# Attention over a context with a routed FFN: the probability product with the probabilities as weights, and a fifth transposing DMA

## The chip, the cores and the metric

The kernel runs on one core of one Trainium2 chip. The time is device microseconds of one execution, from its start to its end. The core has five engines with queues of their own: TensorE (PE; its weight loads are listed as PEld), VectorE (DVE), ScalarE (ACT), GpSimd (POOL) and SyncE (SP), which here only issues DMAs. They wait for one another by semaphores.

## What is computed

Sixteen batches of 128 tokens of width 512; each batch has its own context of 128 tokens of width 256. 32 heads of width 16. The attention, cut to what matters:

```python
q = (layernorm(x) @ Wq).reshape(b, n, 32, 16)
k, v = split(ctx @ Wkv, 2)
q, k = apply_axial_rope(q, pos), apply_axial_rope(k, pos)
w = softmax(einsum('bqhd,bkhd->bhqk', q, k) / 4)
attn = einsum('bhqk,bkhd->bqhd', w, v).reshape(b, n, 512)
x = x + attn @ Wout + bout
x = x + ffn(layernorm(x))     # one shared expert, 16 routed ones, two for each token
```

## The kernel before, in words

The kernel works in fp32 accuracy. Large products are split in two fp16 parts (high and low) of each factor and need three fp16 matmuls (`product`, L501, with `PARTS`); so each matrix that is a factor exists as a high part (made by ScalarE, `..._high`) and a low part (what is left, made by GpSimd or VectorE, `..._low`). The scores are made of such parts as well, with the parts stacked in 64 rows. Only the product of probabilities and values is made in fp32 matmuls.

A batch passes through these parts:

- `ln1_stats`, `ln1_norm` (VectorE), `rstd1_make` (GpSimd), `xn_transpose` (TensorE, L489), `xnT_copy`, `xnT_low`.
- `project_k`, `project_v`, `project_q` (TensorE, L508 to L538), in pieces of three matmuls of 512 columns each: two pieces for K and for V, four for Q. K and Q share the PSUM bank `p_qk`, V and the output projection share `p_v`.
- `k_turn`, `k_sum`, `q_turn`, `q_sum` (VectorE): the rotation. `k_high`, `q_high` (ScalarE), `k_low`, `q_low` (GpSimd) write the fp16 parts in rows, and SP turns them in four transposing DMAs a batch (`turn_parts`, L419), into `kT` and `qT`.
- `scores` (L540, four calls), from which VectorE takes the negative maximum over the keys for each query (`row_max`, L1079, eight calls). `negmax_transpose` (L555) turns them, `neg_copy` copies them, and `shifted_scores` (L564, four calls) makes the scores again, now with keys in the partitions and queries in the free dimension, the maximum taken off by a further matmul. `exp` (ScalarE, L807, eight calls of four heads) writes the fp32 probabilities to `prob`, a ring of four.
- `weigh_values` (L579, four calls of eight heads). The weights of the array are the values of a head, 32 columns wide (16 of them the head's, 16 zeros, in `vpad`), the moving side is `prob`, 128 keys by 128 queries; so the result has the head's dimension in the partitions. Four products for different column groups stand beside each other in the array. As many products again, with `sum_row` as weights, give the sums of the probabilities. ScalarE copies the half (`summed_v_copy`, L813), VectorE inverts the sums (`sums_invert`, L1094), TensorE spreads the inverses over the 16 rows of each head (`spread_recip`, L600, two fp32 matmuls with 128x128 weights) and VectorE multiplies (`normalise`, L1100). So `attn` is already turned, and `attnT_high`, `attnT_low` split it for `project_out` (L606).
- `residual`, `ln2_stats`, `ln2_norm`, `xn2_high`, `xn2_low`, `xn2_transpose`, `xn2T_copy`, `gate_logits`, `keep_logits`: the second norm and the logits of the experts; both forms are stored to DRAM for the FFN.

Every engine has its own loop over steps (`pipeline`, L304), and in it a list, `step(b, on)`, that is written out by hand: `on(d, part)` does the part for batch b + d. So the engines' queues are interleavings of four to six batches in a fixed order, and what is written earlier in an engine's list holds up what comes after it. The lists of TensorE (L643), ScalarE (L881), VectorE (L1169), GpSimd (L1456) and SP (L433) are replaced by the change.

After the attention the eight shared and the routed tiles of the FFN follow (`pair`); the gate and up products of the first shared tile stand in TensorE's last attention step. `project_out(B - 1)` and `hidden_transpose` come behind it. In the last steps ScalarE and VectorE also split the shared weights.

Of the kernel before, what the change touches and what calls it, by code (L numbers as in the profile page):

```python
# [23 lines left out]
F16 = mybir.dt.float16  # L24
# [3 lines left out]
ALU = mybir.AluOpType  # L28
# [3 lines left out]
B = 16  # L32
# [48 lines left out]
def build(nc, x, ctxT, pos, wq, wkv, wo, bout, gateT, gbias, s13, s2, e13, e2, out):  # L81
    with ExitStack() as stack:
# [58 lines left out]
        recip = sb("recip", [P, P])  # L141
        summed_v = sb("summed_v", [P, 2, 3 * P])
        attn = sb("attn", [P, 2, 2 * P])
        attnT = sb("attnT", [P, 2, KC, P], F16)
# [77 lines left out]
        pv_sum = p_pv[:, 2 * P:3 * P]  # L222
# [13 lines left out]
        cleared = sem("cleared"); ident_ready = sem("ident_ready"); consts = sem("consts"); zeroed = sem("zeroed")  # L236
# [16 lines left out]
        pv_done = sem("pv_done"); summed_v_kept = sem("summed_v_kept"); recip_ready = sem("recip_ready")  # L253
        spread_done = sem("spread_done"); attn_ready = sem("attn_ready")

        attnT_hi = sem("attnT_hi"); attnT_lo = sem("attnT_lo"); gate_parts = sem("gate_parts")
# [22 lines left out]
        v_part = vpad.rearrange("p b (m a) d -> p b m (a d)", a=2)  # L279
        v_part = bass.AP(v_part.tensor, v_part.offset, [v_part.ap[0], [HEADS * 2 * HD, 2], [4 * HD, PAIRS], [3 * HD, 2], [1, HD]])  # L280
        attn_rows = attn[:].rearrange("p a n -> p (a n)").rearrange("p (c t) -> p c t", t=P)
# [105 lines left out]
        def _(sp):  # L387
# [44 lines left out]

            def step(b, on):  # L433
                on(-2, turn_k_parts, 0)
                on(-2, turn_q_parts, 0)
                on(-5, store_xn2)
                on(1, load_ctx)
                on(-2, turn_k_parts, 1)
                on(-5, store_xn2T)
                on(-2, turn_q_parts, 1)  # L440
# [47 lines left out]
        def _(pe):  # L488
# [90 lines left out]
            def weigh_values(b, par, i):  # L579

                if i == 0:
# [3 lines left out]
                    else:  # L585
                        pe.wait_ge(consts, 1)
# [3 lines left out]
                block = slice(i % 2 * P, (i % 2 + 1) * P)  # L590
# [950 lines left out]
```

## Time and profile before

| | us |
|---|---|
| median of three timed runs | 694.45 (lowest 692.33, highest 1107.32) |
| the profiled execution | 689.33 |
| its span, first to last instruction | 687.5 |
| TensorE busy | 635.5 (92%) |
| VectorE busy | 503.2 (73%) |
| ScalarE busy | 368.9 (54%) |
| GpSimd busy | 332.9 (48%) |

The profile and the trace tell of one execution. "Busy" is the time in which an engine has an instruction under way; matmuls are pipelined, so it isn't the time in which the array is full. The granted clock is TensorE's, as a share of 2.4 GHz; 0.50 is 1.2 GHz. The attention takes the first 325 us, the FFN the rest.

### The profile page before, as it was taken

What the parts mean: (1) busy time and instruction counts of PE and PEld (TensorE: products, weight loads), DVE (VectorE), ACT (ScalarE), POOL (GpSimd) and SP (SyncE); (2) the same over time, 40 slices, a digit from 0 to 9 for tenths busy, and PEclk for the clock granted to TensorE, in tenths of its full rate; (3) what the DMA queues carried; (4) which work ended last, traced back from release to release, by engine and by line L of the source; (5) the groups of instructions that cost most, each with busy time, mean ns of one, the idle gap of its engine ahead of it and who ended that gap; (6) DMA issues with size and microseconds to landing.
All of it is one profiled execution on the core that took longest, in us unless ns stands there. A gap on an engine that the chain in (4) does not pass through costs nothing.

```text
span 687.5 us, 19434 instructions
## 1 busy us (share of the span) xinstructions
PE 635.5 (92%) x7104; PEld 406.6 (59%) x7104; DVE 503.2 (73%) x976; ACT 368.9 (54%) x620; POOL 332.9 (48%) x390
## 2 busy tenths in 40 slices
PE   2769999999999999988999999999998999999992
PEld 1346666666666666656566566666665666666661
DVE  8779888888888888866486935776765676666671
ACT  4255655666565666566411115665664666666660
POOL 3524555555555555432000012468565478777661
PEclk9989999999999999999999999999999999999997
DMA  9824744544444445650322662665877954555942
GB/s 316 222 48 64 176 112 97 88 94 94 99 99 99 99 99 122 93 125 33 123 92 62 217 210 87 197 197 92 210 219 196 279 111 92 100 85 151 262 77 33
DMA packets 105279, 90.63 MB, mean 132 GB/s; under 512 B 71632, under 2 KB 75728, under 8 KB 105232
## 3 DMA queue, kind: packets, MB, share of 16 engines
q1 hardware_dynamic: 91600, 59.76, 33.4%
q0 software_dynamic: 8752, 20.71, 15.5%
q10 hardware_dynamic: 4880, 9.52, 4.1%
q8 instruction: 31, 0.51, 0.3%
q14 instruction: 16, 0.13, 0.1%
HBM read 69.85 MB, written 22.81 MB: 135 GB/s over the span
## 4 chain that ended last, share of the span: by engine, by line
PE 79%; DMA 5%; DVE 5%; issue 4%; POOL 2%; ACT 2%; SPq 2%; POOLq 0%; ACTq 0%; DVEq 0%
PE p_sc L724 14%; PE p_qk L693 13%; PE p_sc L693 12%; PE p_qk L504 8%; PE p_v L504 8%; PE p_pv L593 4%; PE p_pv L596 3%; DMA used_twice_too<-used_twice 3%; PE p_tr L687 2%; PE p_pv L711 2%; PE p_sc L552 2%; PE p_pv L603 2%; PE p_sc L573 2%; PE p_sc L576 1%; SPq L425 1%
## 5 line engine op out<-in xcount | busy, mean ns | idle before, releaser
L1085 DVE TENSOR_REDUCE negmax<-p_sc 128x4 f16<-128x512 f32 x128 | 79.4, 684 | 6.0 <-PE p_sc L552 4.6
L933 ACT CAST hiddenT<-p_pv 128x384 f16<-128x384 f32 x54 | 25.9, 479 | 107.0 <-PE p_pv L711 103.2
L811 ACT ACTIVATE prob<-p_sc 128x512 f32<-128x512 f32 x128 | 66.1, 602 | 20.2 <-PE p_sc L576 19.9
L1491 POOL DMA_INDIRECT out<-prob,to_at x38 | 69.4, 1826 | 11.1 <-issue 9.7
L724 PE MATMUL p_sc<-used_twice,hiddenT 128*128 128x512 f16 (+1 forms) x306 | 71.7, 379 | 0.9 <-DVE hiddenT L1215 0.9
L1471 POOL COPY from_at<-from_rows 128x1 uint32 (+1 forms) x40 | 33.1, 828 | 80.8 <-DVE from_rows L1330 77.4
L693 PE MATMUL p_qk<-used_twice,xeT 128*128 128x352 f16 x420 | 68.4, 313 | 0.5 <-DMA xeT<-xn2T_dram 0.5
L693 PE MATMUL p_sc<-used_twice,xeT 128*128 128x352 f16 x420 | 68.4, 312 | 0.0
L1211 DVE TENSOR_TENSOR hidden<-p_sc,act_g 128x352 f32<-128x352 f32 x55 | 28.8, 524 | 52.5 <-PE p_sc L693 32.0
L920 ACT COPY xeT<-p_tr 128x1024 f16<-128x1024 f16 x40 | 40.5, 1012 | 37.4 <-PE p_tr L687 35.8
L504 PE MATMUL p_qk<-used_twice,xnT 128*128 128x512 f16 x192 | 52.1, 399 | 6.4 <-DVE swp L1063 6.4
L593 PE MATMUL p_pv<-prob,used_twice_too 128*32 128x128 f32 x1024 | 53.5, 279 | 3.0 <-ACT prob L811 1.8
L1228 DVE TENSOR_SCALAR prob<-p_sc,gate_at 128x512 f32<-128x512 f32 x38 | 28.5, 751 | 37.6 <-PE p_sc L724 30.5
L1442 POOL TENSOR_TENSOR used_twice<-rot,used_twice 128x1024 f16<-128x1024 f32 x16 | 34.2, 2136 | 43.6 <-ACT used_twice L798 43.6
L693 PEld LDWEIGHTS p_sc<-used_twice,xeT 128*128 128x128 f16 x420 | 41.0, 98 | 21.4
L596 PE MATMUL p_pv<-prob,sum_row 128*32 128x128 f32 x1024 | 52.5, 275 | 0.0
L693 PEld LDWEIGHTS p_qk<-used_twice,xeT 128*128 128x128 f16 x420 | 40.8, 98 | 19.4 <-DMA xeT<-xn2T_dram 0.7
L504 PE MATMUL p_v<-used_twice,attnT 128*128 128x512 f16 x192 | 48.9, 380 | 2.6 <-POOL attnT L1450 2.6
L1476 POOL DMA_INDIRECT xe<-xn_dram,from_at x40 | 44.7, 1117 | 8.2 <-issue 4.5
L724 PEld LDWEIGHTS p_sc<-used_twice,hiddenT 128*128 128x128 f16 (+1 forms) x306 | 29.0, 98 | 30.8 <-issue 1.3
L1454 POOL TENSOR_TENSOR xn_parts<-xn,xn_parts 128x512 f16<-128x512 f32 x16 | 18.9, 1179 | 52.9 <-ACT xn_parts L838 52.9
L724 PE MATMUL p_sc<-used_twice_too,hiddenT 128*128 128x512 f16 (+1 forms) x180 | 43.3, 386 | 0.0
(180 smaller groups left out, 1463.6 us busy)
## 6 DMA issues: line engine op xcount, KB each, us to landing
w<-e SPq DMA_DIRECT2D x20, 1408.0 KB
w<-e SPq DMA_DIRECT2D x20, 512.0 KB
out<-stream SPq DMA_DIRECT2D x17, 256.0 KB, 2.0
xn_dram<-xn_parts SPq DMA_DIRECT2D x16, 256.0 KB, 2.2
xn2T_dram<-xn2T SPq DMA_DIRECT2D x16, 256.0 KB, 2.5
w<-e SPq DMA_DIRECT2D x20, 192.0 KB
stream<-x ACTq DMA_DIRECT2D x1, 3584.0 KB, 18.0
xeT<-xn2T_dram ACTq DMA_DIRECT2D x14, 256.0 KB, 2.7
```

The lines of the kernel that those rows point to most:

```text
L504: mm = pe.matmul(to, rows[:, r_part, c, :], w[:, w_part, c, :], start=(c == 0 and r_part + w_part == 0), stop=(c == last and r_part == 1))
L593: pe.matmul(p_pv[2 * HD * n:2 * HD * (n + 1), block], vpad[:, par, head(c, n), :], prob[:, c % RING, n * P:(n + 1) * P], start=(c % 4 == 0 ...
L596: mm = pe.matmul(pv_sum[2 * HD * n:2 * HD * (n + 1), :], sum_row[:, c % 4, :], prob[:, c % RING, n * P:(n + 1) * P], start=False, stop=(c ...
L693: mm = pe.matmul(p_out, xeT[:, u, x_part, c, :], w[:, w_part, c, at:at + INNER], start=(c == 0 and x_part + w_part == 0), stop=(c == KC - ...
L724: mm = pe.matmul(p_y[u][:], hiddenT[0:k, h_part, c, :], w[0:k, w_part, c, :], start=(c == 0 and h_part + w_part == 0), stop=(c == len(ICH) ...
L811: act.activation(prob[:, c % RING, :], p_scored(c)[:], ACT.Exp, scale=SCALE).then_inc(exp_ready, 1)
L920: act.copy(xeT[:, u], p_xT).then_inc(sems.xeT_ready, 1)
L1085: dve.tensor_reduce(negmax[:, c % 2, at:at + CH], p_scored(c)[:].rearrange("p (h t) -> p h t", t=P), AX_X, ALU.max, negate=True).then_inc( ...
L1442: pool.tensor_tensor(q_part[:, :, :, 1, :], twice_each(rot[:, 0:DIM]), q_part[:, :, :, 0, :], ALU.subtract).then_inc(q_parts, 1)
L1471: pool.tensor_copy(from_at[:, par, u:u + 1], from_rows[:, bass.ds(q, 1)]).then_inc(from_copied, 1)
L1476: pool.indirect_dma_start(out=xe[:, u].rearrange("p a d -> p (a d)"), out_offset=None, in_=xn2_dram, in_offset=bass.IndirectOffsetOnAxis(a ...
L1491: pool.indirect_dma_start(out=out, out_offset=bass.IndirectOffsetOnAxis(ap=to_at[:, par, u:u + 1], axis=0), in_=ye[:, par, u], in_offset=N ...
```

## The change

The probabilities become the weights of the array: for each head `prob` (128 keys x 128 queries, fp32) is loaded, and the values of the head with a column of ones, 17 columns (`v_one`), move through. The result `p_heads` has the queries in the partitions, and for each head 16 values and the sum of its probabilities. The products with `sum_row`, `spread_recip` and `summed_v_copy` are gone; VectorE inverts 16 sums a half and multiplies with them spread by the access pattern. `attn` now is in rows; its two fp16 parts (`attn_high` on ScalarE, `attn_low` on GpSimd) are turned by a fifth transposing DMA on SP (`turn_attn`), into one of two buffers of `attnT`. All five lists are written anew. The gate and up products of the first shared tile move behind TensorE's loop.

```diff
-        vpad = used_twice_too[:, 0:4 * DIM].rearrange("p (b h d) -> p b h d", b=2, h=HEADS)
-        sum_row = sb("sum_row", [P, 4, 2 * HD])
-        spread_to = sb("spread_to", [P, 2, P])
+        v_one = used_twice_too[:, 0:2 * HEADS * (HD + 1)].rearrange("p (b h d) -> p b h d", b=2, h=HEADS)
...
+            def turn_attn(b, par):
+                sp.wait_ge(attn_lo, b + 1)
+                if later(b, 2):
+                    sp.wait_ge(wo_done, b - 1)
+                sp.nop().then_inc(turning, 1)
+                sp.dma_start_transpose(attnT[:, par].rearrange("p a c t -> p (a c) t"), attn_parts[:].rearrange("p a d -> p (a d)")).then_inc(attnT_ready, 16)
...
+                on(-3, turn_q_parts, 0)
+                on(-3, turn_k_parts, 1)
                 on(1, load_ctx)
+                on(-3, turn_q_parts, 1)
...
+                on(-5, store_xn2)
+                on(-4, turn_attn)
+                on(-2, turn_k_parts, 0)
+                on(-5, store_xn2T)
...
                 for c in (2 * i, 2 * i + 1):
                     for n in range(CH):
-                        pe.matmul(p_pv[2 * HD * n:2 * HD * (n + 1), block], vpad[:, par, head(c, n), :], prob[:, c % RING, n * P:(n + 1) * P],
-                                  start=(c % 4 == 0), stop=(c % 2 == 1), skip_group_check=True)
-                    for n in range(CH):
-                        mm = pe.matmul(pv_sum[2 * HD * n:2 * HD * (n + 1), :], sum_row[:, c % 4, :], prob[:, c % RING, n * P:(n + 1) * P],
-                                       start=False, stop=(c % 4 == 3), skip_group_check=True)
+                        mm = pe.matmul(p_heads[:, head(c, n) % HALF, :], prob[:, c % RING, n * P:(n + 1) * P], v_one[:, par, head(c, n), :], start=True, stop=True)
                 mm.then_inc(pv_done, 1)
-
-            def spread_recip(b, par, half):
-                pe.wait_ge(recip_ready, b * 2 + half + 1)
-                for n in range(2):
-                    mm = pe.matmul(p_pv[:, n * P:(n + 1) * P], spread_to[:, n, :], recip[:], start=True, stop=True)
-                mm.then_inc(spread_done, 1)
...
             def project_out(b, par, c):
                 if c == 0:
-                    pe.wait_ge(attnT_lo, b + 1)
+                    pe.wait_ge(attnT_ready, b * 16 + 16)
...
```

TensorE's list afterwards, whole:

```python
on(-2, scores, 3)
on(-4, gate_logits)
on(0, xn_transpose)
on(-1, project_v, 1)
on(0, project_k, 0)
on(0, project_k, 1)
on(-3, project_out, 0)
on(-2, negmax_transpose)
on(-3, project_out, 1)
on(-2, shifted_scores, 0)
on(-2, shifted_scores, 1)
on(-3, project_out, 2)
on(-3, project_out, 3)
on(-2, shifted_scores, 2)
on(-2, weigh_values, 0)
on(-2, weigh_values, 1)
on(-2, shifted_scores, 3)
on(0, project_q, 0)
on(-2, weigh_values, 2)
on(-2, weigh_values, 3)
on(0, project_q, 1)
on(-1, scores, 0)
on(-3, xn2_transpose)
on(-1, scores, 1)
on(0, project_q, 2)
on(0, project_q, 3)
on(0, project_v, 0)
on(-1, scores, 2)
```

The others afterwards, shortened to their order (batch offsets of each engine's own step in brackets):

```text
ACT   xnT_copy(-1), v_copy(-2), q_high(-2), exp 0..7(-3), xn2_high(-4), gate_act(0) in step B+2,
      attn_high(-3), xn2T_copy(-4), k_high(-1), ctx_high(0), keep_logits(-4)
DVE   q_sum(-3), neg_copy(-4), ln1_norm(-1), k_turn(-2), residual(-5), ln2_stats(-5),
      sums_invert 0(-4), normalise 0(-4), ln2_norm(-5), k_sum(-2), ln1_stats(0),
      sums_invert 1(-4), normalise 1(-4), split of wo in step 2, row_max 0..3(-3), q_turn(-2),
      row_max 4..7(-3), xnT_low(-1)
POOL  k_low(-2), ctx_low(-1), rstd1_make(0), q_low(-2), bias_add(-3), rstd2_make(-4),
      xn2_low(-4), attn_low(-3)
```

VectorE's part of the product afterwards:

```diff
             def sums_invert(b, par, half):
-                dve.wait_ge(summed_v_kept, b * 2 + half + 1)
+                dve.wait_ge(pv_done, b * 4 + (2 * half + 2))
...
-                dve.reciprocal(recip[:], summed_v[:, half, 2 * P:3 * P]).then_inc(recip_ready, 1)
+                dve.reciprocal(recip[:].rearrange("p (h o) -> p h o", o=1), p_heads[:, :, HD:HD + 1]).then_inc(recip_ready, 1)
 
             def normalise(b, par, half):
-                dve.wait_ge(spread_done, b * 2 + half + 1)
+                dve.wait_ge(recip_ready, b * 2 + half + 1)
...
-                dve.tensor_tensor(attn[:, half], p_pv[:, 0:2 * P], summed_v[:, half, 0:2 * P], ALU.mult).then_inc(attn_ready, 1)
+                dve.tensor_tensor(attn[:, half].rearrange("p (h d) -> p h d", d=HD), p_heads[:, :, 0:HD],
+                                  recip[:].rearrange("p (h o) -> p h o", o=1).broadcast_to([P, HALF, HD]), ALU.mult).then_inc(attn_ready, 1)
```

## Rows read from the trace of the kernel before

**Rows 1.** Windows: one step; busy us (count) by engine, clock, DMA share, GB/s.

```profile
160.00:177.55 17.55, 17.49 (x301) 11.35 (x296) 15.75 (x36) 10.75 (x19) 9.78 (x8) 1.00 0.41 91
```

**Rows 2.** Timeline of TensorE in one step: start us, us, instruction, count.

```profile
163.71 0.61 PE L603 MATMUL p_pv<-recip,spread_to 128*128 128x128 f32 x4
164.25 0.62 PE L552 MATMUL p_sc<-used_twice_too 64*128 64x128 f16 x16
164.81 0.46 PE L504 MATMUL p_tr<-gate,xn2T 128*128 128x16 f16 x12
165.12 0.81 PE L504 MATMUL p_v<-used_twice,ctx 128*128 128x512 f16 x3
...
177.04 0.43 PE L593 MATMUL p_pv<-prob,used_twice_too 128*32 128x128 f32 x8
...
178.92 1.47 PE L504 MATMUL p_qk<-used_twice,xnT 128*128 128x512 f16 x6
```

**Rows 3.** Groups of weight loads, shapes apart: count, busy us, mean ns, idle before.

```profile
L603 PEld LDWEIGHTS p_pv<-recip,spread_to 128*128 128x128 f32 x128 | 17.8, 190 | 10.6 <-DVE recip L1098 8.6
...
L596 PEld LDWEIGHTS p_pv<-prob,sum_row 128*32 128x32 f32 x1024 | 31.6, 111 | 0.0
```

**Rows 4.** Timeline of weight loads where TensorE had been idle: one load; four loads.

```profile
314.20 0.19 PEld L603 LDWEIGHTS p_pv<-recip,spread_to 128*128 128x128 f32 x1 [1.54 <-DVE recip L1098]
...
314.20 0.52 PEld L603 LDWEIGHTS p_pv<-recip,spread_to 128*128 128x128 f32 x4 [1.54 <-DVE recip L1098]
```

**Rows 5.** Timeline of TensorE and VectorE between the two kinds of scores.

```profile
169.59 0.23 PE L573 MATMUL p_sc<-used_twice_too 64*128 64x128 f16 x2
...
176.49 0.62 PE L552 MATMUL p_sc<-used_twice_too 64*128 64x128 f16 x16
...
179.57 0.95 DVE L1098 RECIPROCAL recip<-summed_v 128x128 f32<-128x128 f32 x1 [0.16 <-ACT summed_v L817]
...
181.97 0.42 DVE L1104 TENSOR_TENSOR attn<-p_pv,summed_v 128x256 f32<-128x256 f32 x1 [0.18 <-PE p_pv L603]
...
186.66 0.23 DVE L1092 COPY negmaxT<-p_tr 128x128 f16<-128x128 f16 x1 [0.68 <-PE p_tr L562]
```

**Rows 6.** Groups from 100 to 250 us, and landing of the transposing DMAs.

```profile
L1446 POOL TENSOR_TENSOR used_twice<-rot,used_twice 128x1024 f16<-128x1024 f32 x8 | 17.1, 2138 | 1.2 <-ACT used_twice L805 0.5
...
L1450 POOL TENSOR_TENSOR attnT<-attn,attnT 128x512 f16<-128x512 f32 x8 | 9.3, 1159 | 1.0
...
L805 ACT CAST used_twice<-rot 128x1024 f16<-128x1024 f32 x8 | 8.4, 1048 | 0.0
...
L830 ACT COPY xn2T<-p_tr 128x1024 f16<-128x1024 f16 x8 | 8.1, 1012 | 0.7
...
L1394 POOL TENSOR_TENSOR ctx<-ctx_sb,ctx 128x256 f16<-128x256 f32 x8 | 5.4, 672 | 0.0
...
L823 ACT CAST attnT<-attn 128x512 f16<-128x512 f32 x8 | 5.0, 620 | 4.3 <-DVE attn L1104 4.3
...
DMA to landing us min/median/max: 3.0/3.2/4.8
```

**Rows 7.** Timeline of TensorE: first weighing of batches 0, 13, 15; last output projection.

```profile
45.44 0.65 PE L593 MATMUL p_pv<-prob,used_twice_too 128*32 128x128 f32 x8 [0.42 <-ACT prob L811]
...
277.41 0.43 PE L593 MATMUL p_pv<-prob,used_twice_too 128*32 128x128 f32 x8
...
309.86 0.42 PE L593 MATMUL p_pv<-prob,used_twice_too 128*32 128x128 f32 x8
...
322.63 2.76 PE L504 MATMUL p_v<-used_twice,attnT 128*128 128x512 f16 x12 [0.33 <-POOL attnT L1450]
```

**Rows 8.** Windows at the start and in a late step; columns as in rows 1.

```profile
36.00:42.50 6.50, 0.72 (x4) 0.11 (x2) 6.23 (x11) 2.98 (x7) 0.00 (x0) 0.86 0.00 0
...
45.40:47.20 1.80, 1.76 (x36) 1.79 (x40) 1.42 (x1) 0.87 (x2) 1.44 (x2) 0.50 0.54 104
...
294.20:309.90 15.70, 12.57 (x269) 8.96 (x271) 11.61 (x23) 10.23 (x19) 4.41 (x5) 1.00 0.65 136
```

More of the change, by code:

```diff
@@ L656, in step @@
-                on(-1, project_q, 0)
-                on(-3, spread_recip, 0)
-                on(-1, project_q, 1)
-                on(-2, scores, 0)
-                on(-2, scores, 1)
-                on(-3, weigh_values, 2)
-                on(-3, weigh_values, 3)
-                on(-1, project_q, 2)
-                on(-1, project_q, 3)
-                if isinstance(b, int) and b == B + 2:
-                    pe.wait_ge(turned_q, B * 3)
-                    pe.wait_ge(lo13, KC)
-                    gate(0, 0, 0, 0, "shared")
@@ L769, in pair @@
                             place()
-            pipeline(step, pe, 0, B + 2, 6, (B - 6) // 2, ahead=[xn_transpose])
+            pipeline(step, pe, 0, B + 1, 6, (B - 6) // 2, ahead=[xn_transpose])
+            pe.wait_ge(turned_q, B * 3)
+            pe.wait_ge(lo13, KC)
+            gate(0, 0, 0, 0, "shared")
+            pe.wait_ge(exp_ready, B * NCH)
+            up(0, 0, 0, 0, "shared")
+            gate_logits(B - 2, 0)
             for c in range(KC):
@@ L915, in step @@
                     split_shared13()
+                on(-2, q_high)
+                on(-3, exp, 0)
+                on(-3, exp, 1)
+                on(-3, exp, 2)
+                on(-3, exp, 3)
+                on(-3, exp, 4)
+                on(-3, exp, 5)
+                on(-3, exp, 6)
+                on(-3, exp, 7)
+                if isinstance(b, int) and b == B + 2:
+                    split_shared2()
+                on(-4, xn2_high)
+                if isinstance(b, int) and b == B + 2:
+                    gate_act(0)
+                on(-3, attn_high)
+                on(-4, xn2T_copy)
+                on(-1, k_high)
+                on(0, ctx_high)
+                on(-4, keep_logits)
             def xeT_copy(n, u):
@@ L1169, in step @@
             def step(b, on):
+                on(-3, q_sum)
+                on(-4, neg_copy)
+                if isinstance(b, int) and b == B + 3:
+                    split_shared13((0, 1))
+                on(-1, ln1_norm)
+                on(-2, k_turn)
+                on(-5, residual)
+                on(-5, ln2_stats)
+                if isinstance(b, int) and b == B + 3:
+                    split_shared13((2, 3))
+                on(-4, sums_invert, 0)
+                on(-4, normalise, 0)
+                on(-5, ln2_norm)
+                if isinstance(b, int) and b == B + 3:
+                    split_shared2()
+                on(-2, k_sum)
+                on(0, ln1_stats)
+                on(-4, sums_invert, 1)
+                on(-4, normalise, 1)
+                if isinstance(b, int) and b == 2:
+                    weights_low(wo16, wo_in, KC, KCC + KC)
+                    dve.wait_ge(gate_parts, 1)
+                    dve.scalar_tensor_tensor(gate16[:, 1], gate_sb[:], W_SCALE, gate16[:, 0], ALU.mult, ALU.subtract).then_inc(gate_parts, 1)
+                on(-3, row_max, 0)
+                on(-3, row_max, 1)
+                on(-3, row_max, 2)
+                on(-3, row_max, 3)
+                on(-2, q_turn)
                 on(-3, row_max, 4)
```

153 lines of the change are left out of this document (30 added, 123 removed).

## The prediction

> **What bounds the kernel now.** I read the windows first. In one full step of the attention loop (17.55 us, one batch) TensorE is busy 17.49 us, VectorE 15.75, ScalarE 10.75, GpSimd 9.78, and the granted clock is 1.00, that is 2.4 GHz [rows 1]. The first probability product of batch 0 starts at 45.44 and that of batch 15 at 309.86 [rows 7]: 264.42 us for 15 steps, 17.63 each. So the attention is a row of equal steps bound by TensorE, and VectorE is the next engine. What comes after it (shared and routed experts) isn't touched; it starts when the last output projection is done, so a shift there is taken along to the end.
>
> Then I read TensorE's own order inside a step. Two calls of `weigh_values` (half a batch: 16 products with values and 16 with `sum_row`, two matmul instructions each, 64 in all) run from 177.04 to 178.92: 1.88 us. One `spread_recip` runs from 163.71 to 164.25: 0.54 us [rows 2]. Three matmuls of 512 columns, one piece of a projection, take 3 x 512 columns at 2.4 GHz, 0.64 us, with gaps 0.65.
>
> **What is removed on TensorE.** Two halves at 1.88 and two spreads at 0.54: 4.84 us a batch.
>
> **What is added there.** 32 fp32 matmuls a batch, one for each head, whose weights are the probabilities (128x128) and whose moving side is 17 columns. The trace shows each fp32 matmul as two pairs of weight load and matmul (4 instructions of L603 for 2 matmuls in the source), so 64 pairs. A moving side of 17 columns is nearly nothing: 12 pairs with 16 columns in fp16 run from 164.81 to 165.12, 26 ns a pair [rows 2]. The price is the loading. There the type and the width count: an fp32 load of 128 columns lasts 190 ns, one of 32 columns 111 [rows 3]; the difference, 79 ns for 96 columns, is 0.82 ns a column, 105 ns for 128. The pace shows it directly: where the array had been idle and the loads of L603 began alone, the first load lasts 0.19 us and four of them 0.52, so they start (0.52 - 0.19)/3 = 0.11 us apart, and before the second no matmul was in the way [rows 4]. So 64 x 0.11 = 7.04 us a batch. Bounds: from below 26 ns a pair, as fp16 weights show (1.7 us a batch); from above 190 ns, if a load could not overlap the one before (12.2 us). I take 0.11 us, because it is measured on the same type and width. The old form had hidden this: it loaded 32 columns into one of four column groups at a time, and its instructions passed at 1.88/64 = 29 ns each.
>
> The Trainium skill, in "TensorE: Matmul & The Clock Gate", section "LDWEIGHTS (loading the stationary operand)", puts a load at its columns divided by 1.2 in ns, and its section "Weight-path perf modes" leaves fp32 out of the fast load. That would give 107 ns a load and 6.8 us a batch, against 7.0 by the row. It speaks against the change, since the same section's fast load is what makes 16-column matmuls cheap in fp16.
>
> **Sum on TensorE.** 17.5 - 4.84 + 7.04 = 19.7 us a step. The change takes away multiplications and gives back more in loads: +2.2 us.
>
> **Other engines.** VectorE loses two reciprocals of 128x128 at 0.95 [rows 5], and gets two of 128x16; between an eighth of that, 0.12, by the number of elements, and the old 0.95. I take 0.15; it stands in the rivals alone, since VectorE has slack. ScalarE loses the two copies of `summed_v`. Both had slack. SP gets a fifth transposing DMA: 3.2 us from issue to landing [rows 6]. GpSimd has the same work. None of this is on the path while it is hidden by TensorE; what could bring it there are the two loops that close over a step:
>
> First loop, by way of VectorE. The first shifted scores of a step start at 169.59, so those of the next one a step of 17.55 later, at 187.14; from the first scores (176.49) to them there are 10.65 us now. In this stretch the new order leaves out the reciprocal (0.95 and 0.16 of wait), the normalisation (0.42 and 0.18) and the 0.68 of idle before the copy of the maxima, since `q_sum` now stands there [rows 5]; instructions overlap by some 0.1, so about 8.5 remain. From the first shifted scores (169.59) to the next scores (176.49) there are 6.90 us; the new order has no spread (-0.54), all four weighings instead of the first two (-1.88 + 7.04) and one piece of output projection more (+0.65): 12.2. Together 20.7 us.
>
> Second loop, by ScalarE and GpSimd: after the last weighing come reciprocal and normalisation (together with the matmul's tail some 0.85), `attn_high` 0.62, `xn2T_copy` 1.01, `k_high` 1.05, `k_low` 2.14, `ctx_low` 0.67 [rows 6], and only then `project_k`, since `ctx_low` is now queued behind `k_low`. Together 6.3 us, then two pieces of K (1.3), two of the output (1.3) before the shifted scores, and from them to the end of the last weighing 11.0 (12.2 less the last piece of Q, 0.65, and the gaps): with 0.2 for the handing over 20.1 to 20.2.
>
> Three ways to count the step, 19.7, 20.2 and 20.7; each contains small gaps, the last the most. I take 20.2. The attention output's own chain, `attn_high` 0.62, `attn_low` 1.16, DMA 3.2 [rows 6], ends some 5.2 us after the last normalisation, thus 6.0 after the last weighing. Between the last weighing and `project_out` TensorE has three pieces of Q, two of V, two of K, four of scores, two transposes and the gate product, 6.9 us and its waits; so the new chain is hidden with 1 us to spare, and beyond that it costs what it is late.
>
> **Sum over the kernel.** Thirteen full steps at 20.2 against 17.84 (277.41 - 45.44 over 13) [rows 7]: +30.6. The last two steps lack the projections of a next batch and have idle time already (they take 32.45 us together), so I count +1.5 each: +3. The start: `q_turn` of batch 0 now waits behind the splitting of the output weights, which ScalarE does only after V of batch 0; bounds 0 and +6, since TensorE was busy for only 0.72 of the 6.50 us before its first shifted scores [rows 8]; I take +3, nearer to what VectorE's queue has to take over. The end: from the first weighing of batch 15 to its output projection there are 322.63 - 309.86 = 12.77 us; afterwards it is four weighings and one piece of scores 7.5, transposes and the gate product 2.4, `gate_act` 0.5 (it stands before `attn_high` on ScalarE), 0.62 + 1.16 + 3.2 and hops, 15.6: +2.9. Sum +39.5. On the profiled execution (689.33 us, 687.5 of them span) this is 728.8. The median of the timed runs (694.45) lies 5 us over the profiled execution, of which I count half: **731 us**.
>
> **Rivals.**
> 1. Faster. The two weight sets hide the loads, or the fp32 load runs at the fp16 pace of 26 ns. Then the weighing is 1.7 us, TensorE has 14.4 us of work, VectorE 15.75 - 1.6 = 14.1, and the loops fall to about 15.2: 15 x 2.3 = 35 less, 3 more at the start: about 660. For it: beside these loads the trace has only fp32 matmuls of 128 columns, which could themselves set a pace of about 0.11. Against it: they can't set the first of the three gaps, since the array was empty, and three gaps that make 0.33 together leave no room for a short first one [rows 4]; and the duration grows with the columns [rows 3]. It decides from 75 ns a load down (4.84/64). Chance 0.07.
> 2. No change: a pace between, 80 ns, adds 5.1 and the new order wins a few tenths back; 15 x 0.3 and start and end: about 698. Chance 0.08.
> 3. A wait in the new order: the fifth transposing DMA stands in SP's queue between `store_xn2` and the K transposes, waits there for `attn_low`, and `project_out` gets its rows late; one landing took 4.8 us [rows 6]. At 1.5 us a step more, +22: 752. For it: only 1 us of slack. Against it: the queue has nothing else due just then. Chance 0.15.
> 4. The clock. In a weighing the array would multiply for 17 columns once or twice, 7 to 14 ns at 2.4 GHz, in each 110. After the stretch in which TensorE had been busy for 0.72 of 6.50 us the granted clock was 0.50 (1.2 GHz), from 45.4 to 47.2, up to 4.7 us after the end of that stretch [rows 8]. If the two weighing stretches of a step, 3.5 us each, count as idle, each costs half of some 4 us: 2 x 2 x 15 = 60: 790. Against it: through the last steps, with TensorE busy 80% of the time, the clock stays at 1.00 [rows 8]. Chance 0.10.
>
> The same page of the Trainium skill, "TensorE: Matmul & The Clock Gate", Part 4, says that transposes don't count as activity for the gate; no run here shows how loads count. By that, rival 4 would be likelier than I put it.
>
> **How the numbers follow.** My forecast has 0.60; its own range is 712 to 748 (steps of 19.6 to 20.9, start and end from 0 to 10). Low end 708, high end 764: this takes in rival 3 and leaves out rivals 1, 4 and part of 2. A measurement of this kernel tells about 2% (14 us) from no change, so faster means under 680, slower over 708: faster 0.07, same 0.08, slower 0.85.
>
> **What would show it.** Right: 64 loads of 128 columns fp32 a batch, 190 ns each and 0.11 apart, a weighing quarter of 1.76 us where it was 0.94; a step of 20.2 us with VectorE under 80% busy; `project_k` waiting for `ctx` from GpSimd, or the shifted scores for VectorE's maxima, under 1 us a step. Wrong: a pace of loads under 75 ns; steps under 17.6; a granted clock of 0.50 inside the steps; or a wait for the DMA of the attention rows before the output projection above 1 us a step.

## The result, and where the time went

The change made the kernel slower by 30%: 900.29 us (median of 4 runs, 895.06 to 901.07) against 693.39, a ratio of 1.298 with an interval of 1.292 to 1.304. That is not the 731 that was forecast, and not in its range. The profiled execution took 900.32, of which 898.3 are span; the granted clock over the whole span is 0.86 where it was 0.98.

Below are the head, two bands and four groups of the page after the change. Columns of the groups: count, then busy us and mean ns, then the idle time of the engine before them and what ended it.

```profile
span 898.3 us, 17096 instructions
...
PE 770.2 (86%) x5952; PEld 508.7 (57%) x5952; DVE 493.1 (55%) x976; ACT 355.6 (40%) x588; POOL 328.3 (37%) x382
...
PE   4387788779777977969999889999999989999994
...
PEclk9768798788878875677678679999999989999997
...
L593 PEld LDWEIGHTS p_pv<-used_twice_too,prob 128*128 128x128 f32 x1024 | 146.6, 230 | 6.0 <-issue 1.3
...
L555 PE MATMUL p_sc<-used_twice_too 64*128 64x128 f16 x512 | 33.9, 290 | 73.2 <-DMA used_twice_too<-used_twice 72.4
...
L1077 DVE RECIPROCAL recip<-p_pv 128x16 f32<-128x16 f32 x32 | 8.2, 257 | 104.1 <-PE p_pv L593 104.1
```

Two things stand in it that the forecast's sum has at zero. In the first 24 of the 40 slices, which are the attention, the clock moves between 0.5 and 0.9. And the first scores of the steps (L555) waited 72.4 us for a DMA that brings the turned Q and K.

The windows between the marks of [rows 7] put the loss in its place: start, 13 steps, the last two steps, the last output projection's wait, and the rest. Columns: busy us (count) of the five engines, clock, DMA share, GB/s.

```profile
0.00:55.42 55.42, 25.29 (x147) 10.91 (x148) 37.08 (x81) 20.28 (x32) 17.60 (x31) 0.85 0.55 171
55.42:457.15 401.73, 331.16 (x2857) 227.98 (x2853) 196.27 (x434) 129.00 (x219) 122.63 (x102) 0.79 0.32 68
457.15:507.19 50.04, 46.41 (x409) 34.48 (x405) 21.41 (x48) 18.19 (x31) 13.04 (x11) 0.69 0.35 77
507.19:528.09 20.90, 17.45 (x128) 14.62 (x125) 7.11 (x17) 7.57 (x13) 3.63 (x3) 0.76 0.14 38
528.09:898.30 370.21, 349.88 (x2424) 220.75 (x2424) 231.20 (x399) 180.57 (x294) 171.41 (x237) 0.97 0.56 144
```

| stretch | before [rows 7] | after | more | forecast |
|---|---|---|---|---|
| start, to the first weighing | 45.44 | 55.42 | 10.0 | 3 |
| 13 steps | 231.97 | 401.73 | 169.8 | 30.6 |
| last two steps | 32.45 | 50.04 | 17.6 | 3 |
| to the last output projection | 12.77 | 20.90 | 8.1 | 2.9 |
| after it | 364.87 | 370.21 | 5.3 | 0 |

Nine tenths of the loss are the steps (187.4 of 210.8 us): 30.9 us each (401.73/13) instead of 17.84, where 20.2 was forecast.

Now one step. First TensorE's timeline; each line has the start, the length, the instruction and, in brackets, the idle time before it.

```profile
209.80 3.75 PE L593 MATMUL p_pv<-used_twice_too,prob 128*128 128x17 f32 x32
...
214.69 3.64 PE L593 MATMUL p_pv<-used_twice_too,prob 128*128 128x17 f32 x32
...
218.18 1.07 PE L507 MATMUL p_qk<-used_twice,xnT 128*128 128x512 f16 x3
...
222.90 0.81 PE L507 MATMUL p_v<-used_twice,ctx 128*128 128x512 f16 x3
...
229.75 1.22 PE L555 MATMUL p_sc<-used_twice_too 64*128 64x128 f16 x16 [6.05 <-DMA used_twice_too<-used_twice]
```

The weighing itself is what was forecast: 32 pairs in 3.64 to 3.75 us, 0.11 us a pair and little more. But then compare the projections: three matmuls of 512 columns have 0.81 in [rows 2], and so has V at 222.90; the same in Q at 218.18 take 1.07. The windows of the same stretch say why (the last six columns as above):

```profile
209.80:213.60 3.80, 3.80 (x41) 3.77 (x39) 1.37 (x6) 1.08 (x2) 0.55 (x1) 1.00 0.76 175
...
214.70:218.20 3.50, 3.50 (x34) 3.50 (x34) 1.68 (x6) 1.03 (x3) 1.16 (x1) 1.00 0.39 75
218.20:223.60 5.40, 5.40 (x38) 2.50 (x37) 3.76 (x7) 2.88 (x4) 1.93 (x2) 0.68 0.01 3
223.60:229.70 6.10, 0.11 (x1) 0.00 (x0) 0.85 (x3) 0.00 (x0) 2.48 (x3) 0.93 0.42 108
229.70:231.00 1.30, 1.25 (x19) 0.80 (x20) 0.60 (x1) 0.00 (x0) 0.00 (x0) 0.50 1.16 187
231.00:234.00 3.00, 2.55 (x20) 1.60 (x20) 2.31 (x5) 0.77 (x2) 0.00 (x0) 0.50 0.04 6
```

Read the clock beside TensorE's busy time. TensorE is counted busy for the whole of both weighings, yet the clock falls at their end, to 0.68 on the mean of the next 5.4 us, and comes back. Then TensorE stands for 6 us, and once more the clock is at 0.50 (1.2 GHz) for what follows.

The wait is explained by the chain of waits, start and length, one step of it without pieces under 0.15 us:

```profile
214.85 3.49 PE p_pv L593 x32
218.37 0.27 DVE recip L1077
218.66 0.44 DVE attn L1083
219.19 0.63 ACT attn_parts L804
219.89 1.15 POOL attn_parts L1422
221.04 1.75 issue
222.82 0.31 POOL used_twice L1418
223.13 1.78 issue
224.91 0.67 POOL ctx L1374
225.84 0.41 SPq L412
226.38 3.26 DMA used_twice_too<-used_twice
229.75 1.22 PE p_sc L555 x16
```

The chain says "issue" (the engine waited for nothing that the profile shows) where the timelines of ScalarE and GpSimd have more:

```profile
220.79 1.01 ACT L811 COPY xn2T<-p_tr 128x1024 f16<-128x1024 f16 x1 [0.98 <-PE p_tr L619]
222.82 2.13 POOL L1418 TENSOR_TENSOR used_twice<-rot,used_twice 128x1024 f16<-128x1024 f32 x1 [1.78 <-ACT used_twice L792]
```

`k_low` (L1418) is one instruction of 2.13 us, which the chain cuts in two, and it waited 1.78 us for `k_high` (L792). That stands in ScalarE's list behind `xn2T_copy` (L811), which waited 0.98 us for the transposes that TensorE makes after the weighing, one piece of Q and one call of `scores`. So the weighing's end leads by two branches, VectorE's and TensorE's own list, over ScalarE and GpSimd to `ctx_low` (L1374). What waits for it is not only `project_k` but SP: `load_ctx` of a later batch (L412) stands in SP's new list between `turn_k_parts 1` and `turn_q_parts 1`, and so the transpose of Q's second part, whose data are long there, is issued after it. With 3.26 us from issue to landing the scores come 6 us late. This is a loop over the step (scores, exponentials, weighing, `xn2_transpose` and `attn_high`, `xn2T_copy`, `k_high`, `k_low`, `ctx_low`, `load_ctx`, `turn_q_parts 1`, scores), so the delay isn't caught up.

### The profile page after: what moved, and what is told of

Read it like the earlier page. It is cut to its first block, busy times and chain, and to the rows that moved or that the text cites. A ratio compares the mean times of both kernels' runs of the same rounds, so it can differ in the third digit from the quotient of the medians.

```text
span 898.3 us, 17096 instructions
## 1 busy us (share of the span) xinstructions
PE 770.2 (86%) x5952; PEld 508.7 (57%) x5952; DVE 493.1 (55%) x976; ACT 355.6 (40%) x588; POOL 328.3 (37%) x382
## 4 chain that ended last, share of the span: by engine, by line
PE 68%; DMA 11%; issue 10%; POOL 5%; ACT 3%; DVE 2%; SPq 1%; POOLq 0%; ACTq 0%; DVEq 0%
PE p_pv L593 14%; PE p_sc L705 11%; PE p_qk L674 10%; PE p_sc L674 9%; PE p_v L507 7%; PE p_qk L507 5%; DMA used_twice_too<-used_twice 5%; PE p_sc L576 2%; DMA stream<-x 2%; PE p_sc L555 2%; PE p_tr L668 2%; PE p_pv L692 2%; PE p_sc L579 2%; DMA xeT<-xn2T_dram 2%; PE p_tr L499 1%
## 5 line engine op out<-in xcount | busy, mean ns | idle before, releaser
L593 PEld LDWEIGHTS p_pv<-used_twice_too,prob 128*128 128x128 f32 x1024 | 146.6, 230 | 6.0 <-issue 1.3
L593 PE MATMUL p_pv<-used_twice_too,prob 128*128 128x17 f32 x1024 | 146.8, 293 | 0.5 <-DVE attn L1083 0.5
L555 PE MATMUL p_sc<-used_twice_too 64*128 64x128 f16 x512 | 33.9, 290 | 73.2 <-DMA used_twice_too<-used_twice 72.4
L555 PEld LDWEIGHTS p_sc<-used_twice_too 64*128 64x128 f16 x512 | 21.5, 124 | 95.9 <-issue 60.9
L674 PE MATMUL p_qk<-used_twice,xeT 128*128 128x352 f16 x420 | 70.2, 318 | 2.3 <-DMA xeT<-xn2T_dram 2.3
L507 PE MATMUL p_qk<-used_twice,xnT 128*128 128x512 f16 x192 | 66.9, 487 | 4.1 <-DVE swp L1042 4.1
L1077 DVE RECIPROCAL recip<-p_pv 128x16 f32<-128x16 f32 x32 | 8.2, 257 | 104.1 <-PE p_pv L593 104.1
L1191 DVE TENSOR_TENSOR hidden<-p_sc,act_g 128x352 f32<-128x352 f32 x55 | 28.8, 524 | 57.8 <-PE p_sc L674 38.0
L507 PE MATMUL p_v<-used_twice,attnT 128*128 128x512 f16 x192 | 50.7, 399 | 5.1 <-DMA attnT<-attn_parts 4.4
L674 PEld LDWEIGHTS p_sc<-used_twice,xeT 128*128 128x128 f16 x420 | 41.1, 98 | 21.6
L1422 POOL TENSOR_TENSOR attn_parts<-attn,attn_parts 128x512 f16<-128x512 f32 x16 | 18.5, 1154 | 83.9 <-ACT attn_parts L804 83.9
```

The source lines that it names most:

```text
L507: mm = pe.matmul(to, rows[:, r_part, c, :], w[:, w_part, c, :], start=(c == 0 and r_part + w_part == 0), stop=(c == last and r_part == 1))
L555: mm = pe.matmul(p_scored(2 * cc + a)[:, n * P:(n + 1) * P], qT[rows, CH * cc + n, :], kT[rows, CH * cc + n, :], start=True, stop=True)
L593: mm = pe.matmul(p_heads[:, head(c, n) % HALF, :], prob[:, c % RING, n * P:(n + 1) * P], v_one[:, par, head(c, n), :], start=True, stop=True)
L674: mm = pe.matmul(p_out, xeT[:, u, x_part, c, :], w[:, w_part, c, at:at + INNER], start=(c == 0 and x_part + w_part == 0), stop=(c == KC - ...
L1191: dve.tensor_tensor(hidden[:, 0:INNER], p_u, act_g[:], ALU.mult).then_inc(sems.hidden_ready, 1)
```

## The experiments

The theories before the runs: A, the wait in SP's queue is the loss and the clock follows from the idle time it makes; B, the long loads with hardly a multiplication let the clock fall by themselves, wait or none; with, for the forecast's terms, questions of the order of the work and of the type of the loads.

**1. `load_ctx` at the end of SP's list.**

```diff
                 on(-3, turn_k_parts, 1)
-                on(1, load_ctx)
                 on(-3, turn_q_parts, 1)
...
                 on(-5, store_xn2T)
+                on(1, load_ctx)
```

> The changed kernel with one line moved: SP's load_ctx stands at the end of SP's list and no longer ahead of the second Q transposes, which waited there for ctx_low. Theory A (the queue is the cause, and the idle 6 us a step are what lowers the clock): the wait for the DMA before scores 2 is gone, steps of 20.2 us, granted clock 1.00 inside the steps, in all about 750 us. Theory B (the two weighing stretches lower the clock by themselves, because the array hardly multiplies there): the wait is gone, but the clock still falls to 0.50 after or inside a weighing stretch in each step, steps of 23 to 27 us, in all 790 to 840 us.

It took 844.64 us, 55.7 less and a little above what B expected, with the clock at 0.856, as in the changed kernel (0.861). TensorE waits for no turned Q any more and is busy 29.11 us of 30, and still its clock is 0.77 there:

```profile
150.00:180.00 30.00, 29.11 (x259) 20.49 (x258) 17.30 (x40) 11.04 (x20) 12.37 (x11) 0.77 0.40 74
```

The step is 26.6 us ((449.04 - 50.05)/15, first weighings). Where the clock is low inside the weighing, the loads suffer too. TensorE's timeline of this kernel, two successive weighings, and 2-us windows (busy, clock, DMA share, GB/s) of TensorE alone:

```profile
186.51 3.75 PE L593 MATMUL p_pv<-used_twice_too,prob 128*128 128x17 f32 x32
...
192.15 6.85 PE L593 MATMUL p_pv<-used_twice_too,prob 128*128 128x17 f32 x32
```

```profile
192.00:194.00 2.00, 2.00 (x11) 0.50 0.88 171
...
204.00:206.00 2.00, 2.00 (x30) 0.95 0.16 29
```

The same 32 pairs take 3.75 us at 1.00 and 6.85 at 0.50: 214 ns a pair instead of 110. Against the changed kernel the edit wins 5.4 us before the first weighing and 3.5 in each of the 15 steps (26.6 against (507.19 - 55.42)/15 = 30.1), and loses 2.5 behind them. Theory A falls as the whole: without the idle time the clock is as low as with it.

**2. The engines' lists of before, with the new product.** All five lists in the old order, no `spread_recip`; the four pieces of `project_out` stand behind the first two shifted scores, and `turn_attn` goes between `turn_k_parts 0` and `turn_q_parts 0` (SP's list, shortened):

```diff
             def step(b, on):
-                on(-3, turn_q_parts, 0)
-                on(-3, turn_k_parts, 1)
+                on(-2, turn_k_parts, 0)
+                on(-4, turn_attn)
+                on(-2, turn_q_parts, 0)
+                on(-5, store_xn2)
                 on(1, load_ctx)
...
```

> The new product and the fifth transposing DMA with the five lists of the kernel before; only the output projection is moved behind the first shifted scores, to give the DMA its 3 us, and the fifth DMA stands between K's and Q's first transposes. Theory A (new order is the cause): no long wait for a DMA, clock 1.00, steps of about 20 us by the loads alone, in all about 735 us. Theory B (the product lowers the clock in any order): steps of 23 to 27 us, in all 780 to 840 us.

904.97 us, with a clock of 0.848; both theories had less, 735 and 780 to 840, since neither counted a wait for the fifth DMA in this order. Here TensorE waits in most steps for the turned attention rows, as rival 3 had it (which I had named for the new order, where it doesn't occur):

```profile
205.35 4.15 PE L507 MATMUL p_v<-used_twice,attnT 128*128 128x512 f16 x12 [4.82 <-DMA attnT<-attn_parts]
```

So the new order does what it is for: it takes the fifth transpose off the path. With the old one the product costs as much as with the new one and its wait.

**3. The new order with the old product**, on the kernel before (`load_ctx` last; where `spread_recip` and the copies of `summed_v` go is my own placing):

```diff
+                on(0, project_q, 0)
+                on(-2, spread_recip, 0)
...
+                on(0, project_q, 2)
+                on(-2, spread_recip, 1)
+                on(0, project_q, 3)
```

> The kernel before with the five new lists (load_ctx last on SP), but its own product: 32-column weights, sum_row, spread_recip (between the first two pieces of Q, and after the third), summed_v_copy, no fifth DMA. Theory B (only the product is slow, the new order is harmless once load_ctx is out of the way): clock 1.00, steps of 17.5 to 18.5 us, 690 to 715 us. Rival (the new order is itself slower, its loops close later): steps over 19 us, over 720 us.

753.73 us, ratio 1.087 (1.080 to 1.095); the step is 21.6 us. My forecast for it missed, and the rival was right: the order loses time with the old product. TensorE is busy 44.35 of 50 us at a clock of 0.97; it waits for the reciprocal before the spreads and for `logits` before the transposes:

```profile
215.82 0.71 PE L603 MATMUL p_pv<-recip,spread_to 128*128 128x128 f32 x4 [1.59 <-DVE recip L1097]
...
219.78 0.63 PE L496 MATMUL p_tr<-ident,xn 128*128 128x128 f32 x4 [1.01 <-ACT logits L866]
```

It doesn't say what the order alone costs, since another placing of the spreads might wait less. It does show that the order isn't free when the product between is another.

**4. Twice the moving columns.** Each head's matmul takes 32 columns (its own 17 and what lies beside them, which nobody reads) instead of 17; on experiment 1.

```diff
-        v_one = used_twice_too[:, 0:2 * HEADS * (HD + 1)].rearrange("p (b h d) -> p b h d", b=2, h=HEADS)
+        v_one = used_twice_too[:, 0:2 * HEADS * 2 * HD].rearrange("p (b h d) -> p b h d", b=2, h=HEADS)
...
-        p_heads = p_pv[:, 0:HALF * (HD + 1)].rearrange("p (h d) -> p h d", d=HD + 1)
+        p_heads = p_pv[:, 0:HALF * 2 * HD].rearrange("p (h d) -> p h d", d=2 * HD)
```

> As e1_ctx_last, with 32 columns of values moving where 17 moved (the columns beyond the one of ones are not used): twice the multiplying for the same loads and the same waits. Theory A: as e1_ctx_last within 1%. Theory B: the stretch counts for more in the clock, so it falls less often or later, 10 to 60 us faster than e1_ctx_last; the same time would say that twice this little isn't enough, and would leave B standing only if the clock falls at the same places.

840.54 us, clock 0.858: the same. The mean load is 265 ns (269 in experiment 1), and the second weighing of a step again takes 6.9 us in all steps but one. The columns themselves are free, as they should be behind a load of 110 ns, and the clock is no better for 15 more of them.

**5. Loads in fp16.** Probabilities and values in fp16, on experiment 1:

```diff
-                        mm = pe.matmul(p_heads[:, head(c, n) % HALF, :], prob[:, c % RING, n * P:(n + 1) * P], v_one[:, par, head(c, n), :], start=True, stop=True)
+                        mm = pe.matmul(p_heads[:, head(c, n) % HALF, :], prob16[:, c % RING, n * P:(n + 1) * P], v_one[:, par, head(c, n), :], start=True, stop=True)
```

> As e1_ctx_last, with probabilities and values rounded to fp16 (the low parts of both are left out), so that a head's product is one load and one matmul in fp16 instead of two and two in fp32. Both theories: a pair takes 26 to 30 ns, the weighing 1 us a batch instead of 7, the clock stays at 1.00, steps of 15.5 to 17 us by VectorE and the loops, in all 655 to 690 us. If the new order alone were slow, it would stay over 700.

690.54 us, 154 less than experiment 1 and just above the 655 to 690 expected. The timeline of TensorE and a window of this kernel:

```profile
207.48 0.56 PE L594 MATMUL p_pv<-used_twice_too,prob 128*128 128x17 f16 x16
```

```profile
180.00:210.00 30.00, 27.21 (x359) 15.12 (x357) 26.29 (x61) 19.27 (x33) 17.88 (x15) 1.00 0.50 114
```

Sixteen products in 0.56 us, 35 ns each with the end of the last one, where the fp32 form has 32 pairs in 3.75; and the clock is 1.00 in the window. The whole loss hangs on the type of the product, which sets both how long a load takes and how many there are. This isn't the changed kernel made whole again, since the low parts of the products are left out.

**6. A filler: more work, to hold the clock.** On experiment 1, behind each head's product one matmul of 240 columns of zeros in fp16, into columns of `p_pv` that nobody reads: 512 more matmuls.

```diff
                         mm = pe.matmul(p_heads[:, head(c, n) % HALF, :], prob[:, c % RING, n * P:(n + 1) * P], v_one[:, par, head(c, n), :], start=True, stop=True)
+                        mm = pe.matmul(p_pv[:, 512 - 240:512], ident16[:], filler[:], start=True, stop=True)
```

> As e1_ctx_last (844.6 us), with a matmul more behind each head's product: 128x128 weights in fp16, 240 columns of zeros moving, written beside the heads' results and read by nobody; 512 matmuls more in all. It runs while the next fp32 weights are loaded. Theory B (the weighing lowers the clock because the array hardly multiplies in it): the clock stays at 1.00 in the steps, a head takes 0.24 to 0.33 us instead of 0.22 at full and 0.43 at half clock, steps of 21 to 24 us instead of 26.6, in all 750 to 800 us: more work, less time. Rival (the fp32 loads themselves or the power lower the clock): the clock falls as before and the filler only adds, 850 to 880 us.

771.86 us: 72.8 less than the same kernel without the 512 matmuls. The windows of the steps, and the loads:

```profile
150.00:200.00 50.00, 49.11 (x579) 35.19 (x577) 32.58 (x79) 22.66 (x38) 21.33 (x18) 1.00 0.49 94
200.00:250.00 50.00, 48.66 (x588) 33.98 (x586) 34.99 (x81) 22.89 (x40) 22.79 (x20) 1.00 0.38 84
```

```profile
L594 PEld LDWEIGHTS p_pv<-used_twice_too,prob 128*128 128x128 f32 x1024 | 135.5, 195 | 5.2 <-issue 1.6 <-DVE attn L1085 1.2
```

The clock is 1.00, the mean load 195 ns over the whole kernel (269 in experiment 1, and [rows 3] have 190), and the step 21.7. The rival, that the fp32 loads or the power lower the clock, expected 850 to 880 and falls. The filler also brings 512 loads of its own, in fp16; experiment 10, which has the same loads and differs from this one in the moving columns alone, shows that more moving columns by themselves win 34.4 of the 72.8 us; how the rest divides between the filler's loads and its first 128 columns isn't shown. With both, theory B stands as the cause of the clock's part: how much the array multiplies between the loads.

**7. A lighter start**, on experiment 5: the splitting of the output weights moved to the end of step 2 on ScalarE, and to step 3 on VectorE (VectorE's part of the edit).

```diff
-                if isinstance(b, int) and b == 2:
+                if isinstance(b, int) and b == 3:
                     weights_low(wo16, wo_in, KC, KCC + KC)
```

> As e5_fp16 (690.5 us; low parts of probabilities and values left out), with the splitting of the output weights moved back behind the first batch's work on ScalarE (to the end of step 2) and VectorE (to step 3). If what e5 loses at its start (its first weighing at 51.7 us, before at 45.4) comes from that splitting: first weighing near 47, in all 684 to 687 us. If it comes from something else: as e5 within 2 us.

695.07 us, ratio to the kernel before 1.007 (1.002 to 1.012). The first weighing starts at 54.24, later than the 51.74 without the edit. But the experiment doesn't clear the splitting, since the edit moved it from one place on the path to another. TensorE's timeline, then VectorE's:

```profile
27.56 1.46 PE L508 MATMUL p_qk<-used_twice,ctx 128*128 128x512 f16 x6 [3.78 <-DVE swp L1043]
...
44.26 0.61 PE L556 MATMUL p_sc<-used_twice_too 64*128 64x128 f16 x8 [4.68 <-DVE negmax L1065]
...
38.62 4.16 DVE L1026 SCALAR_TENSOR_TENSOR used_twice<-w,used_twice 128x512 f16<-128x512 f32 x4 [5.17 <-ACT used_twice L832]
```

In experiment 5 the same wait for `q_turn` (L1043) is 7.19 us and the first scores start at 38.55; here it is 3.78 and they start at 35.26. So the splitting ahead of `q_turn` does cost 3.3 us of the start. Then it is paid back: the splitting now stands ahead of the first `row_max`, waits there 5.17 us for ScalarE's part of it, and the next scores wait 4.68 us for the maxima.

**8. The kernel before, with fp16 probabilities, values and `sum_row`**; low parts left out as in experiment 5.

```diff
-        vpad = used_twice_too[:, 0:4 * DIM].rearrange("p (b h d) -> p b h d", b=2, h=HEADS)
-        sum_row = sb("sum_row", [P, 4, 2 * HD])
+        vpad = used_twice_too[:, 0:2 * DIM].bitcast(F16).rearrange("p (b h d) -> p b h d", b=2, h=HEADS)
+        sum_row = sb("sum_row", [P, 4, 2 * HD], F16)
```

> The kernel before, its order and its form of the product, with probabilities, values and sum_row in fp16 (the low parts of probabilities and values are left out). It is the fair partner of e5_fp16: what the same rounding brings where 32-column weights stand beside each other. The product falls from 3.8 to about 1 us a batch on TensorE, so VectorE's 15.75 us bound the step: 16 to 16.6 us a step, in all 665 to 678 us, faster than before and than e5_fp16 (690.5). Rival (the old order's loop by way of VectorE sets the step, not TensorE): steps of 17 to 17.5, 685 to 692 us.

684.29 us, ratio 0.990 (0.985 to 0.994). The forecast was lower and the rival nearly right. The windows show whose limit comes next:

```profile
150.00:200.00 50.00, 46.75 (x686) 26.34 (x686) 45.68 (x103) 32.67 (x57) 28.52 (x25) 1.00 0.45 102
```

TensorE has some 3 us of 50 free, and VectorE is busy 45.68 of them: 91%. The old product leaves VectorE near its limit. Experiment 5 has taken VectorE's two large reciprocals away and its 15 steps take 16.8 us each ((303.96 - 51.74)/15; from batch 7 on 16.3), shorter than these 17.1; what it wins there it pays at the start, where its first weighing comes 5.4 us later (51.74 against 46.31), and at the end. Of all versions only this one is measurably faster than the kernel before, by 1%, at the price of precision.

**9. The filler on the changed kernel itself**, with `load_ctx` where the change has it. The edit is that of experiment 6.

> The changed kernel (900.3 us, load_ctx where the change put it) with the filler of e6_filler. Theory B with the wait as a second, separate cause of lost clock: the fall behind the second weighing is gone, the one after the idle 6 us stays, steps of 21.7 + 6 + 1 to 3 = 29 to 30.5 us against 30.9, in all 870 to 895 us. Rival (the idle time alone never lowers the clock, only idle time and weighing together): clock 1.00 throughout, steps of 27.5 to 28, 845 to 860 us.

871.64 us. The time is where theory B with a second cause had it (870 to 895), the steps a little over its 29 to 30.5. The wait for the turned Q is there again, up to 6.9 us long, and the steps with it are 30.7. The clock through the wait, TensorE alone:

```profile
218.00:220.00 2.00, 2.00 (x29) 1.00 0.00 0
220.00:222.00 2.00, 1.58 (x8) 1.00 0.00 0
222.00:224.00 2.00, 0.00 (x0) 0.96 0.00 0
224.00:226.00 2.00, 0.00 (x0) 0.50 0.21 63
```

After the weighing, the filler holds the clock at 1.00 (0.68 without it); through the idle time it can't, and it falls all the same. The steps to batch 9 take as long with the filler as without (first weighing of batch 9 at 330.97 and 332.38). In batch 5 one sees why: from the first weighing to the end of the second the filler takes 9.4 us instead of 8.5, and from there to the scores 10.6 instead of 11.4; TensorE's own work in between is shorter, and its wait longer by some of that (6.58 instead of 6.05). It wins only behind that: the changed kernel's next two steps take 37.1 and 35.4 us at clocks of 0.63 and 0.71, those with the filler 30.8. The last four steps have no wait in either kernel, since no context is left to load, and there the filler wins 4.1 us a step (21.5 against 25.6).

**10. A smaller filler**, 128 columns instead of 240, otherwise experiment 6.

> As e6_filler (771.9 us) with 128 filler columns for each head where 240 moved. Theory B, if this much multiplying still holds the clock: a head takes no longer than in e6_filler (0.25 us) and perhaps 0.24, clock 1.00 in the steps, 764 to 772 us. If it doesn't hold it: the clock falls in the steps again, and the time lies between e6_filler and e1_ctx_last, 790 to 840 us.

806.28 us, half way between 771.86 and 844.64, with steps that alternate between 21.6 and up to 27.7 us:

```profile
200.00:250.00 50.00, 49.10 (x516) 35.88 (x515) 28.97 (x68) 20.75 (x36) 19.02 (x16) 0.86 0.37 81
```

In some steps the clock falls, in others it holds.

## Why the prediction was wrong

The four kernels with and without the wait, with and without the filler, are the answer in one table (us):

| | `load_ctx` in the middle | at the end |
|---|---|---|
| no filler | 900.29 | 844.64 |
| filler | 871.64 | 771.86 |

Three of these are single runs; the kernel before took 692.98, 693.18 and 690.78 beside them, and from their last weighing on, where the four do nearly the same work, they take between 384.0 and 389.1 us, so differences of tens of us don't come from the chips. The two causes aren't additive: one remedy alone wins 55.7 or 28.7, both together 128.4. Each makes the clock fall, and while one of them is there the other's remedy is partly idle. By the step: 17.6 us before; with the loads at full clock 20.8; with the fall of the clock 26.6; with the wait 30.7 (batches 1 to 9; 30.9 over the first 13 steps, 30.1 over all 15). The 20.8 is experiment 6's 21.7 less the filler's own time: 14 heads took 3.48 us there (209.00 to 212.48), 0.249 each against 0.22 for two loads, so 32 x 0.029 = 0.9; that is an estimate, and no run has the loads at full clock without a filler.

Point by point:

- **The price of a load, 0.11 us: right.** 64 x 0.11 = 7.04 a batch; the trace after has 3.75 and 3.64 for its halves, and the duration is the 190 ns of [rows 3] where the clock is full. Rival 1 (loads hidden) falls. Rival 2 (80 ns) too.
- **The step at that price, 20.2: nearly right**, if the clock and the queue had been as the sum took them: 20.8. For the whole kernel experiment 6 gives an estimate: 771.86 less the filler's 16 x 0.9 is 757, inside the range of the forecast, some 26 above its value.
- **The first step that failed: the clock.** The sum multiplied durations of the full clock throughout, and the clock stood outside it as rival 4 with 0.10. Its mechanism is what happened: the weighing counts for little, and what follows runs at half the clock. Two things made me put it low. I took the last steps of before, with TensorE at 80% and a clock of 1.00 [rows 8], as the nearest row; but there the busy time is mostly multiplying, and in a weighing of 17 columns it is mostly loading. And the price I gave (2 us for each weighing, 4 a step, 790 in all) left out that the load itself slows down with the clock: a weighing at 0.50 takes 6.85 us instead of 3.75, 3.1 more. Measured it is 5.8 us a step (26.6 less 20.8). A page of the Trainium skill, "TensorE: Matmul & The Clock Gate", has in its section "HAM oscillation — how this bites in real kernels" the case of a narrow matmul that lets the clock fall in every round, puts it down to the DMA wait in the round, and gives padding as one way out. Experiment 1 differs from it in that the clock is 0.77 with TensorE busy 97% and no DMA wait; experiment 6, more columns for nobody's use, is near to that way out and agrees with it. I should have weighed it, and cited only its sentence on transposes.
- **The second step that failed: the order of SP's list.** In rival 3 I wrote that the queue has nothing else due just then, and looked for the wait at the transpose of the attention rows. The second loop that I drew went through `ctx_low` to `project_k` and stopped there (I counted 6.3 us from the weighing to `ctx_low`'s end, and it took 7.2, 218.33 to 225.57, with a wait for TensorE's transposes that I hadn't); the same `ctx_low` also releases `load_ctx`, and what stands behind `load_ctx` in SP's list, `turn_q_parts 1`, was due. Its price, experiment 1 against the changed kernel: 55.7 us, 3.5 a step. Here the question had been put (a wait that is added: who is queued behind it?) and answered for one queue of the two that wait for the same semaphore.
- **The attention rows' own chain: right.** It is hidden in the steps of the new order and shows only at the very end (3.01 us before the last output projection, in the 8.1 of the table above); in the old order it costs 4.8 us a step (experiment 2).
- **The start, +3: mis-sized.** It is +10.0. 5.4 of it is the queue again, which I hadn't counted: with `load_ctx` last the first weighing starts at 50.05. The rest, 4.6, is in the new order and not in the product: the new product in the old order starts at 45.49 (experiment 2), the old product in the new order at 51.87 (experiment 3). TensorE's K of batch 1 waits 7.33 us there for `q_turn` of batch 0, and the first scores start at 38.00 instead of 30.86. What I gave for it, `q_turn` behind the splitting of the output weights, is one part: experiment 7 shows 3.3 us, though its edit paid them back elsewhere. The other part I hadn't counted: in VectorE's new list `q_turn` also stands behind `ln1_stats` of a later batch, which waits for its input; so it starts at 28.82 instead of 21.14. VectorE's timeline of the changed kernel:

```profile
25.26 0.69 DVE L983 BATCH_NORM_STATS2 stats<-stream 128x6 f32<-128x512 f32 x1 [4.12 <-DMA stream<-x]
```

How the 7.1 us at the first scores shrink to 4.6 at the weighing was not followed up. Beside it the first steps are dear in themselves: from the first weighing of batch 0 to that of batch 1 experiment 1 takes 28.8 us, with its first weighings at half the clock.
- **VectorE's small reciprocal**: 257 ns, not the 150 I took. It has slack; nothing follows.
- **After the attention, 0**: 5.3 us more at a clock of 0.97 instead of 0.98. The first 10 us of it run at 0.83, where before they had 1.00; the rest was not followed up.

## What to carry to other kernels

Count what the array multiplies, not how long TensorE is busy. A change of roles that puts the large operand into the weights and leaves few columns moving costs twice: the loads, whose pace and number the type sets, and then the clock, which falls under a TensorE that every row calls busy; when a sum uses durations from a full clock, ask which stretches of the new kernel multiply as little as the idle stretches of the old one. And when a new order puts an instruction later, go through every queue that waits for its semaphore, and in each look at what stands behind the waiting instruction: here it was a prefetch, needed by nobody for a long time, that held up the transfer that everybody waited for.

## What was new about the hardware

- More work made the kernel faster: 512 matmuls of zeros, 72.8 us less (experiments 1 and 6). With 128 columns in each instead of 240 the gain is 38.4 us.
- The granted clock fell to 0.50 in stretches in which TensorE was counted busy for 97% and more of the time (experiment 1: 0.77 on the mean of 30 us, 0.50 in the window from 192 to 194 with TensorE busy throughout); neither the busy share nor the idle time before the low stretch gave it away.
- An fp32 load of 128 columns follows the clock: 0.11 us at 2.4 GHz, 0.214 at 1.2. Loads of the same size in fp16 went by at 35 ns a product, matmul included.
- The two weight loads of an fp32 product can't be told from the source, which has one matmul: 512 of them are 1,024 loads in the trace, and each half pays the full 128 columns.
